# A two-layer cross-attention kernel: expert weights waited for apart, expert loops written out, output transposes of 36 columns and later in the window, ternary weights in the last unit

## The reference, cut to what matters

```python
def _L0_xattn_ref(latents, tokens, ...):      # x 8x56x128, context 8x1500x128, 16 heads of 8, 8 experts
    q = _ln(latents, sa_ln_g, sa_ln_b)
    x = latents + _mha(q, q, ...)                            # self-attention
    x = x + _mha(_ln(x, ...), _ln(tokens, ...), ...)         # cross-attention, 1500 keys
    h = _ln(x, moe_ln_g, moe_ln_b)
    vals, idx = top_k(h @ rw.T + rb, 2)
    h1 = gelu(einsum('nd,efd->enf', h, fc1_w) + fc1_b)       # all 8 experts, 512 wide
    eo = einsum('enf,edf->end', h1, fc2_w) + fc2_b
    return x + (gates of the two best experts) * eo
def _L1_xattn_ref(x, context, ...):
    # cross-attention again, with Wq, Wk, Wv, Wo rounded to -1, 0, 1 times the mean of abs(W)
    return residual + (out @ bit_quant(Wo).T + bo)
x = _L0_xattn_ref(x, ctx, ...); x = _L1_xattn_ref(x, ctx, ...)
```

## Time and profile before

| what | value |
|---|---|
| median of 3 runs | 633.04 us (632.65 to 633.94) |
| profiled execution | 633.05 us, of which 631.3 us are its span |
| mean granted TensorE clock | 0.929 of full speed |
| PE busy | 542.5 us |
| DVE busy | 389.0 us |
| ACT busy | 326.4 us |
| POOL busy | 199.1 us |

### The profile page before, as it was taken

The page is one execution under the profiler, slowest core; times in us unless marked ns, Lnnn a source line. Parts: engine busy times, 40 slices in busy tenths (PEclk is TensorE's granted clock), DMA queues, the critical chain, the costliest instruction groups (busy, mean ns, idle before and its releaser), DMA issues.

```text
span 631.3 us, 16157 instructions
## 1 busy us (share of the span) xinstructions
PE 542.5 (86%) x6582; PEld 386.4 (61%) x6582; DVE 389.0 (62%) x974; ACT 326.4 (52%) x495; POOL 199.1 (32%) x190
## 2 busy tenths in 40 slices
PE   0699838799999999979968989378999999999996
PEld 0587515566666767747736767145666766767774
DVE  5668479677777776776234211578777677676720
ACT  1265214456767677635733333225666666666572
POOL 2553214647594854400025100224041240330000
PEclk9899769889999999979987999778999999999997
DMA  5010621634554435412200731026537437353300
GB/s 155 34 51 1 164 76 44 166 75 128 136 130 117 130 77 145 93 50 57 100 1 3 177 108 60 25 69 153 132 91 185 119 86 178 86 144 84 72 3 16
DMA packets 36987, 58.66 MB, mean 93 GB/s; under 512 B 16308, under 2 KB 20524, under 8 KB 36916
## 3 DMA queue, kind: packets, MB, share of 16 engines
q1 hardware_dynamic: 36916, 57.66, 36.1%
HBM read 17.81 MB, written 0.23 MB: 29 GB/s over the span
## 4 chain that ended last, share of the span: by engine, by line
PE 54%; issue 23%; DVE 11%; DMA 5%; POOL 3%; ACT 2%; SPq 2%; DVEq 0%; POOLq 0%; ACTq 0%
PE SM L1209 11%; PE PO L1224 11%; PE ST L1181 7%; PE MI L1123 6%; PE MI L1133 6%; DVE mxp L824 5%; PE MI L1157 2%; PE MI L1112 2%; DMA cx<-in_ctx 2%; PE SM L1296 2%; DMA qst<-mrow 1%; ACT ksplit L598 1%; PE SM L1157 1%; DVE cstat L796 1%; SPq L361 1%
## 5 line engine op out<-in xcount | busy, mean ns | idle before, releaser
L824 DVE TENSOR_REDUCE mxp<-SM 112x1 f32<-112x500 f32 x364 | 237.5, 674 | 92.0 <-PE SM L1209 91.2
L626 ACT ACTIVATE PT<-ST 128x896 f32<-128x896 f32 x192 | 171.3, 912 | 57.7 <-PE ST L1181 57.5
L1209 PE MATMUL SM<-kst,qst 96*112 96x500 bf16 x364 | 141.5, 403 | 16.8 <-DVE mxp L824 12.5
L1181 PEld LDWEIGHTS ST<-qst,kst 98*128 98x128 bf16 x1536 | 94.8, 100 | 37.2 <-issue 13.6
L1181 PE MATMUL ST<-qst,kst 98*128 98x112 bf16 x1536 | 108.9, 215 | 1.8 <-DMA qst<-mrow 1.8
L500 POOL TENSOR_TENSOR kr<-kf,ksplit 128x500 f32<-128x500 f32 x48 | 54.3, 1134 | 149.3 <-ACT ksplit L598 149.3
L1224 PE MATMUL PO<-PT,vaug 125*32 125x112 f32 x3072 | 98.0, 266 | 2.1 <-ACT PT L626 1.5
L1224 PEld LDWEIGHTS PO<-PT,vaug 125*32 125x32 f32 x3072 | 71.7, 111 | 24.9 <-issue 16.2
L1209 PEld LDWEIGHTS SM<-kst,qst 96*112 96x112 bf16 x364 | 46.9, 131 | 48.8 <-DVE mxp L824 31.8
L610 ACT ACTIVATE vaug<-MI 125x512 f32<-125x512 f32 x48 | 28.7, 598 | 77.4 <-PE MI L1133 77.4
L505 POOL TENSOR_TENSOR ksplit<-kr,ksplit 128x500 bf16<-128x500 f32 x48 | 54.6, 1138 | 41.7 <-DVE ksplit L819 41.7
(11 more groups left out here) (131 smaller groups left out, 544.0 us busy)
## 6 DMA issues: line engine op xcount, KB each, us to landing
kst<-ksplit SPq DMA_DIRECT2D x192, 187.5 KB, 3.8
cx<-in_ctx SPq DMA_DIRECT2D x8, 750.0 KB
xT<-in_ctxT SPq DMA_DIRECT2D x8, 750.0 KB, 5.1
moe<-in_w1T SPq DMA_DIRECT2D x8, 256.0 KB, 2.9
moe<-in_w2T SPq DMA_DIRECT2D x8, 256.0 KB, 3.0
qall<-qsplit SPq DMA_DIRECT2D x12, 112.0 KB, 2.3
qst<-qall SPq DMA_DIRECT2D x56, 21.0 KB, 1.9
watt<-in_watt SPq DMA_DIRECT2D x1, 768.0 KB, 5.3
```

Source lines behind the costliest of these rows:

```text
L626: nc.scalar.activation(PT[:, k % PTB], ST[:, k % 2, :, 0:4 * PC], ACT.Exp, scale=SCALE).then_inc(exp_done, 1)
L824: nc.vector.tensor_reduce(mxp[:, j // 3, j % 3:j % 3 + 1], tile_bank(j, banks), AX.X, ALU.max).then_inc(sm_red, 1)
L1181: last = mm(ST[:, k % 2, cc, PC * p:PC * (p + 1)], kst[n.par][:, 4 * half + p, at:at + 128], qst[n.par][:, 4 * half + p], start=True, stop ...
L1209: mm(tile_bank(j, banks), qst[n.par][0:SROWS, j // 3], kst[n.par][0:SROWS, j // 3, at:at + THIRD], start=True, stop=True).then_inc(sm_full, 1)
```

## The change

There are four edits. (1) The two weights of an expert have a semaphore each. `load_w1(e)` waits for the last fc1 of expert e-2, `load_w2(e)` for its last fc2; PE waits for w1 ahead of fc1 and for w2 ahead of fc2. In SP's queue expert 3's second weight now stands behind the two restacks. (2) The expert loops on SP, PE, ACT and DVE are written out. (3) `transpose_po` picks the 36 wanted columns, so that its output is packed; it moves from k=3 to k=7, its normalising on DVE to k=8, and forth from k=7 to k=9. (4) `ternary_weights` moves to unit c=7, k=0.

```diff
-K_STEP, BACK_STEP, V_STEP, FORTH_STEP, CTX_STEP = 0, 3, 4, 7, STEPS - 3
+K_STEP, V_STEP, BACK_STEP, FORTH_STEP, CTX_STEP = 0, 4, 7, 9, STEPS - 3
...
+            def load_w1(e):
+                if e >= 2:
+                    sp.wait_ge(fc1_full, (e - 1) * CPE)
+                sp.dma_start(w1s[e % 2], ...).then_inc(ld_w1[e % 2], 16)
+            def load_w2(e):
+                if e >= 2:
+                    sp.wait_ge(fc2_step, (e - 1) * CPE)
+                sp.dma_start(w2s[e % 2], ...).then_inc(ld_w2[e % 2], 16)
...
-            sp.wait_ge(fc2_step, CPE)
-            load_expert(2, 0)
-            sp.wait_ge(fc2_step, 2 * CPE)
-            load_expert(3, 1)
+            load_w1(2)
+            load_w2(2)
+            load_w1(3)
             restack(v0, 0)
             restack(v0, 1)
-            with sp.Fori(1, 3) as it:
-                for j in range(2):
-                    sp.wait_ge(fc2_step, it * (2 * CPE) + (j + 1) * CPE)
-                    load_expert(it * 2 + (j + 2), j)
+            load_w2(3)
+            for e in range(4, E):
+                load_w1(e)
+                load_w2(e)
...
-                heads = bank[0:L].rearrange("q (h x) -> q h x", x=32)
+                heads = back[0:L, 0:H * VW].rearrange("q (h x) -> q h x", x=VW)
...
-                    if k == BACK_STEP and (n + -1).exists():
+                    if k == BACK_STEP + 1 and (n + -1).exists():
                         normalise_unit(n + -1)
...
-                    if n.s == 0 and n.c == B - 3 and k == HSTEP:
+                    if n.s == 0 and n.c == B - 1 and k == 0:
                         ternary_weights()
...
+                rows_of = ident[:].rearrange("k (p x) -> k p x", x=32)
                 for half in range(2):
                     for hh in range(2):
-                        at = 256 * half + (128 - VW) * hh
-                        last = mm(bank[0:L, at:at + 128], po[:, PC * half + L * hh:PC * half + L * (hh + 1)],
-                                  ident[:], start=True, stop=True, skip_group_check=True)
+                        at = 4 * VW * (2 * half + hh)
+                        last = mm(back[0:L, at:at + 4 * VW], po[:, PC * half + L * hh:PC * half + L * (hh + 1)],
+                                  rows_of[:, :, VW * hh:VW * (hh + 1)], start=True, stop=True,
+                                  skip_group_check=True)
...
                     if c == 0:
-                        pe.wait_ge(ld_exp[j], it * 32 + 32)
+                        pe.wait_ge(ld_w1[j], it * 16 + 16)
...
+                    if c == 0:
+                        pe.wait_ge(ld_w2[j], it * 16 + 16)
...
-            with pe.Fori(1, E // 2) as it:
+            for it in range(1, E // 2):
                 experts(it)
```

More of the change, by code:

```diff
@@ L270, in build_kernel @@
         ld_xT = [sem(f"ld_xT{i}") for i in range(2)]
-        ld_exp = [sem(f"ld_exp{i}") for i in range(2)]
+        ld_w1 = [sem(f"ld_w1{i}") for i in range(2)]
+        ld_w2 = [sem(f"ld_w2{i}") for i in range(2)]
         padded, v_ones = sem("padded"), sem("v_ones")
@@ L349, in _ @@
                              mask_in[hh * DH, H:H + 2].partition_broadcast(DH * TERMS)).then_inc(ld_member, 16)
-            def load_expert(e, j):
-                sp.dma_start(w1s[j], w1T_in[bass.ds(e, 1)].rearrange("a i f -> (a i) f")).then_inc(ld_exp[j], 16)
-                sp.dma_start(w2s[j], w2T_in[bass.ds(e, 1)].rearrange("a f c d -> (a f) c d")).then_inc(ld_exp[j], 16)
+            def load_w1(e):
+                if e >= 2:
+                    sp.wait_ge(fc1_full, (e - 1) * CPE)
+                sp.dma_start(w1s[e % 2], w1T_in[bass.ds(e, 1)].rearrange("a i f -> (a i) f")).then_inc(ld_w1[e % 2], 16)
+            def load_w2(e):
+                if e >= 2:
+                    sp.wait_ge(fc2_step, (e - 1) * CPE)
+                sp.dma_start(w2s[e % 2], w2T_in[bass.ds(e, 1)].rearrange("a f c d -> (a f) c d")).then_inc(
+                    ld_w2[e % 2], 16)
             def load_qall(n):
@@ L416, in window @@
                 if n.s == 0 and n.c in (3, 4):
-                    load_expert(n.c - 3, n.c - 3)
+                    load_w1(n.c - 3)
+                    load_w2(n.c - 3)
             u0, u1 = Unit(0, None, 0), Unit(0, None, 1)
@@ L728, in gelus @@
                     act.wait_ge(fc1_full, it * (2 * CPE) + (i + 1))
-                    if not isinstance(it, int) or i >= CPE:
+                    if it or i >= CPE:
                         act.wait_ge(fc2_step, it * (2 * CPE) + (i + 1 - CPE))
@@ L734, in _ @@
             gelus(0)
-            with act.Fori(1, E // 2) as it:
+            for it in range(1, E // 2):
                 gelus(it)
@@ L851, in place_q, with normalise @@
                 last.then_inc(qst_ready, 1)
-            def normalise(bank, full, rden_sem, done, full_at, rden_at, par):
+            def normalise(back, full, rden_sem, done, full_at, rden_at, par):
                 dve.wait_ge(full, full_at)
-                heads = bank[0:L].rearrange("q (h x) -> q h x", x=32)
+                heads = back[0:L, 0:H * VW].rearrange("q (h x) -> q h x", x=VW)
                 nc.vector.reciprocal(rden[:], heads[:, :, DH]).then_inc(rden_sem, 1)
@@ L1068, in _ @@
             dve.wait_ge(b2_added, 1)
-            with dve.Fori(1, E // 2) as it:
+            for it in range(1, E // 2):
                 add_experts(it)
@@ L1149, in transpose_max, with transpose_po @@
                                     identb[0:PC, 0:PC]).then_inc(mx_full, 1)
-            def transpose_po(bank):
+            def transpose_po(back):
+                rows_of = ident[:].rearrange("k (p x) -> k p x", x=32)
                 for half in range(2):
                     for hh in range(2):
-                        at = 256 * half + (128 - VW) * hh
-                        last = mm(bank[0:L, at:at + 128], po[:, PC * half + L * hh:PC * half + L * (hh + 1)],
-                                  ident[:], start=True, stop=True, skip_group_check=True)
+                        at = 4 * VW * (2 * half + hh)
+                        last = mm(back[0:L, at:at + 4 * VW], po[:, PC * half + L * hh:PC * half + L * (hh + 1)],
+                                  rows_of[:, :, VW * hh:VW * (hh + 1)], start=True, stop=True,
+                                  skip_group_check=True)
                 return last
@@ L1412, in fc2 @@
                     pe.wait_ge(gelu_done, it * (2 * CPE) + (i + 1))
-                    if i == 0 and isinstance(it, int):
+                    if c == 0:
+                        pe.wait_ge(ld_w2[j], it * 16 + 16)
+                    if i == 0 and it == 0:
                         pe.wait_ge(lg_ready, 1)
-                    if c == 0 and not isinstance(it, int):
+                    if c == 0 and it:
                         pe.wait_ge(expert_added, it * 2 + (j - 1))
@@ L1426, in experts @@
                     fc2(i)
-                    if isinstance(it, int) and i == CPE - 1:
+                    if it == 0 and i == CPE - 1:
                         transpose_gates()
```

## The result

The changed kernel takes 626.82 us (median of 4 runs, 624.15 to 634.0) against 632.85 (4 runs) for the kernel before on the same chip; the ratio is 0.9863 [0.9818, 0.9908]. The changed kernel is faster, by 6.0 us in the medians and by 8.7 by the ratio (its interval reaches from 5.8 to 11.5), and not by the 24.3 forecast; 608.8 and the range from 603.5 to 616 are both missed. The profiled execution took 626.4 us against the 633.05 that the sum was made against: 6.65 less.

What follows compares the result with a forecast made beforehand. PE was taken to bound the kernel, busy 542.5 of 631.3 us. Gains of 3.5 + 5.8 + 6.7 + 0.3 + 8.0 = 24.3 us off 633.05 gave 608.8 us, range 603.5 to 616.

Steps and rivals of the forecast that it cites:

- the short call's duration: Output transposes of 36 columns: a call costs 0.50 us instead of 1.08, so 0.58 saved.
- The rival of the branch: Experts: the wait at 368.71 was the loop branch, so written-out loops remove 2.7 us: 606.4 us, chance 0.05.
- 6 times 0.58 is 3.5 us: Self-attention: of eight shorter output-transpose calls about six count, 0.58 us each, 3.5 us gained.
- The ternary term: Pass 0, unit c=5: moving the ternary weights removes 3.95 us of wait and 2.73 of slow clock, 6.7 us gained.
- Of 1.4 us gained up to there 0.45 are left: Pass 0, units c=1 to 3: PE meets DVE at the return, leaving 0.45 us gained each, 1.35 in all.
- Net 1.15 us a unit: Pass 1 units: shorter call and moved output together gain 1.15 us each, about half from the call; bounds 0.58 and 1.6.
- the upper bound: Output transposes: a short call costs at most 0.77 us, from a row of 16 fp32 matmuls in 1.54 us.
- So a wait of 2.2 to 2.7 us replaces one of 2.72: I take 0.2 gained: Experts: PE waits for expert 3's second weight instead of expert 4's; 0.2 us gained, from 0.5 lost to 1.5 gained.
- The last call of pass 1: Behind the last unit of pass 1: the output-transpose call standing alone there gains 0.58 us.
- The wait comes back at steps 7 to 9: Rival: PE meets DVE or ACT late at the return in every unit; 613.6 us, or 616, chance 0.20.
- The last rival: Whole kernel: the gains of the moves vanish and only the ternary weights' gain comes; 626 us, chance 0.02.
- the slower rival: Output transposes: strided identity reads make each call slower; 3.2 us a call gives 645 us or so, chance 0.03.

Runs made afterwards that it cites:

- experiment 4: Changed kernel with expert 3's second weight loaded between the two restacks, not behind both: 621.41 us, ratio 0.9828.
- experiment 2: Self-attention's output transposes alone: 128 columns in the changed kernel, 621.39 us; 36 columns in the kernel before, 636.98 us; also the changed kernel rerun, 627.81 us.
- experiment 3: Changed kernel with DVE's normalising of a context in self-attention spread over two steps: 621.51 us, ratio 0.9821.
- experiment 1: Each part alone on the kernel before: ternary weights ratio 0.9913, 36 columns 0.9929, places 1.0032, expert weights and loops 0.9994.
- the last kernel of 6: Changed kernel with spread normalising in self-attention, expert 3's second weight between the restacks, context loads of windows 1 to 3 later: 617.1 us, ratio 0.9722.

## Why the prediction was wrong

Right in mechanism and size: the ternary weights (6.66 for 6.7), the short call's duration (0.53 for 0.50), a wait for DVE at the return in pass 0's first units, the wait of 2.2 to 2.7 us moving from expert 4 to expert 3 (2.36), and the weight, not the branch, as the cause of the wait: it stood at expert 3 with the loops written out, and went with the place of one load (experiment 4). The rival of the branch is out. That the loops cost nothing at all rests on the turn without a gap in the earlier trace rows; they were never written out alone. The Trainium skill, "Runtime: NRT & Kernel Launch", section "Instruction fetch mechanics", says that a taken branch can stall an engine; these traces give the wait to the weight. No read by groups of nine was slow.

**"6 times 0.58 is 3.5 us" in self-attention: -3.77 came.** This is the largest error, 7.3 us. The step counted waits at one clock. It saw PE wait 0.94 us for DVE and called the shorter call hidden there; hidden it is, but the wait becomes 1.87. Of the 0.93 more, 0.48 are the shorter call and 0.46 a cast on DVE that took 0.86 us for 0.40 (last section). The clock that fell behind it cost 4 us in this trace, and 0 to 4 in others (experiments 2, 3). The ternary term had priced just this effect, in the same trace, from the earlier trace rows; I did not ask the question again where the change makes PE wait longer.

**"Of 1.4 us gained up to there 0.45 are left" in units c=1 to 3 of pass 0: -0.23, -0.96, -0.95 came.** The step walked PE, DVE and ACT but not the transfers. In the kernel before, PE came to the tile of step 4 about when the keys landed (it waited 0.25 us there in unit c=1); PE arriving a microsecond earlier only waits for them, as the places alone show (experiment 1), and the move's return at k=9 costs its 0.35 and a 0.40 wait on top. With the context load out of the way the units are 0.6, -0.05 and 0.6 shorter than before, 1.16 in all; in the other five traces with that load moved they gained 0.4 to 0.9 in all. The forecast was 1.35.

**"Net 1.15 us a unit" in pass 1: 0.75 came.** Of it 0.48 is the call (experiment 1), taken as 0.58; the last call of pass 0, alone on the path, gave 0.48 too. I had read the long call as its piece of 1.08 in the chain. In the timeline of self-attention before, PE's next piece starts 1.02 after it, and 1.02 less the 0.53 of the short call is 0.49. (The row behind the upper bound, 16 products in 1.54 us, is a piece that the chain cut short; at full clock the same 16 take 1.71 in the chain. Nothing came of it, since the call measured 0.53.)

```profile
50.43 1.08 PE L1157 MATMUL SM<-ident,po 128*56 128x128 f32 x8
51.45 1.78 PE L1296 MATMUL SM<-qr,qbd 128*112 128x56 f32 x16
```

The moves gave 0.28 instead of 0.57. PE's idle time per unit was some 0.68 us (24.32 busy of 25.00), and is 0.26 (23.94 of 24.20), in windows of the length of a unit before and after:

```profile
478.00:503.00 25.00, 24.32 (x357) 17.39 (x356) 17.72 (x35) 16.76 (x26) 6.72 (x6) 1.00 0.52 128
480.00:504.20 24.20, 23.94 (x355) 16.94 (x356) 18.33 (x35) 16.55 (x25) 6.73 (x6) 1.00 0.54 131
```

A move changes no work of PE, so it can give back PE's idle time in the unit and no more: 0.57 would have needed nearly all of the 0.68. The later units fell short likewise: 0.77, 0.76, 0.47 and 0.48 for 1.05, 1.15, 0.85 and 0.8 in pass 0.

**"So a wait of 2.2 to 2.7 us replaces one of 2.72: I take 0.2 gained": -1.26 came.** The wait is right. Whether the clock falls behind it differs from execution to execution: not in the trace of before, nor with this part alone (68.87 us); it did in the changed kernel and its repeat (71.12, 70.92), and, with the old wait at expert 4, with the places alone (70.90). The price of such a wait is 2.4 us plus a clock loss of 0 to some 1.7 (the 4.04 of experiment 4 less 2.36).

**The last call of pass 1: -0.33 for 0.58.** The stage behind the last unit took 7.6 to 9.0 us in the traces with long calls there and 8.2 to 8.5 in those with short ones. It is settled by when the clock falls while PE is nearly idle. Before, the two products of the return took 0.42 us and the eight pieces of the projection 0.47 twice and then 0.77; in the changed kernel they took 0.64 and 0.77 eight times, 0.82 us more, which eats the 0.48 of the call and 0.34 besides. What sets that moment stays open.

**Rivals.** "The wait comes back at steps 7 to 9" comes nearest for pass 0, though the wait that decides there is at step 4, for keys; its 613.6 still left self-attention its gain. The last rival, the gains of the moves gone and ternary's kept, had 626 and a chance of 0.02. The measured time is that number, and it is luck: the call and the moves gained 4.9 us in pass 1's units, and self-attention and the experts lost 5.0. In the slower rival the sum is wrong: 3.2 us a call is 22 times 2.7 or 59 us above the forecast, not 645. None of my cases had the clock take back a gain.

Open stays unit 0 of pass 0. From the end of self-attention it took 66.3 and 66.4 us in the two traces of the changed kernel, 69.3 in two others with the same order there (experiments 2, 4), and 65.4 in the one of experiment 3. In one of those of 69.3, a wait for the maxima's rows, which queue behind the restack, is followed by slow products (8 of 128 columns in 1.91 us instead of the 1.07 of the earlier trace rows):

```profile
129.32 0.93 PE L1193 MATMUL ST<-qst,kst 98*128 98x112 bf16 x8 [3.01 <-DMA qst<-mrow]
...
132.71 1.91 PE L1143 MATMUL MI<-watt,xT 128*125 128x128 f32 x8
```

The changed kernel had the same wait (3.43 us) and was back at full clock 3 us after it; its repeat waited 1.16 us there, with the same instructions. PE has one more wait for no engine at 112 to 117 us in each. The two add up to 5.4 and 5.5 us where the unit took 69.3, and to 3.5 to 4.7 where it took 65.4 to 66.4. So part of the spread is how long these transfers take (the last kernel of 6, with 4.2 and 68.2, fits less well). Why one execution waits less or recovers sooner was not found, and an order with the rows ahead of the restack was not tried.

## What to carry to other kernels

When a change shortens PE's work in a stretch where another engine is the longer path, what it saves turns into idle time of PE, and that can cost the clock behind it: price each PE wait that grows, not only those that vanish, and look for what on the other engine can be moved out of that wait first. A step moved earlier meets the transfers as well as the engines: before crediting the gain, list what each piece on the new path waits for from DMA, with the time at which it landed, and do the same for the first unit, where the order that helps the steady ones may be too late. Where several items are queued on SP, the cheapest gain may be the order of two loads: one line was worth 2 to 4 us here.

## What the runs showed of the hardware

The granted clock after the same wait is not the same in every execution. In the window from 56.5 to 65 us, behind PE's wait of 1.87 us in self-attention, it was 0.50, 0.54, 0.57, 0.58, 0.60 and 0.80 in six traces (experiment 2), with waits of 0.85 and 0.94 us it was 0.99 and 1.00. One trace of a kernel is one draw of this: stage times there scatter by 4 us with the same instructions.

DVE's cast of `kr` takes 0.41 us alone and up to 1.34 beside POOL; the one of 0.86 at 51.38 us makes up half of what the wait in self-attention grew by. All 48 casts together took 30.5 us of DVE (20.2 before), so they account for the 9.7 us by which its busy time grew. It comes with the shift in timing, which lays casts beside POOL's instructions: 29.7 us with the places alone and 25.9 with the short calls alone, 20.4 and 20.5 with the ternary weights and the expert part alone. Timeline of a pass-1 unit, DVE and POOL:

```profile
488.89 1.34 DVE L829 CAST ksplit<-kr 128x500 bf16<-128x500 f32 x1 [0.17 <-POOL kr L510]
...
488.81 1.14 POOL L515 TENSOR_TENSOR ksplit<-kr,ksplit 128x500 bf16<-128x500 f32 x1
```

The cast ends at 490.23, 0.28 us after POOL's instruction at 489.95. The Trainium skill, "SBUF — State Buffer", section "SBUF: two separate sides", says that DVE and GpSimd have one pair of ports in common, held for a whole instruction by GpSimd, or by DVE where its instruction is in a two-port mode or has two inputs in SBUF, while the other blocks. This trace is in keeping with it, and so is the cast of 0.86, which ended at 52.24, 0.28 us after POOL's instruction at 51.96. That the cast is in such a mode no row shows, and no run here took POOL's work away.
